# Layer-2 attention: the choice of keys in two DVE steps, the residual added by POOL, the values spread by ACT

## The chip, the cores and the metric

The kernel runs on one core of one Trainium2 chip. The metric is the device time of the whole program, in microseconds (us). The program is a chain of eight layers; the change touches one of them, the attention of layer 2, which takes some 390 us of the span, from about 1682 to about 2070 us.

## The reference, cut to what matters

`x` has 8192 tokens of 128 channels (128 sequences of 64), `ctx` as many. The layer's attention works within one sequence, with 16 heads of 8 channels, and its result is added to `x`:

```python
x = x + _L2_xattn_ref(_layernorm(x, axis=-1), ctx_1024, Wq, Wkv, Wc)

def _L2_xattn_ref(q, kv, Wq, Wkv, Wc):
    qp = einsum('bld,ed->ble', q, Wq)
    idx = argmax(einsum('bld,bmd->blm', qp, kv), axis=-1)   # one context row for each token
    mk, mv = split(einsum('bld,ed->ble', take(kv, idx), Wkv), 2, axis=-1)   # 8 key, 8 value channels
    attn = softmax(einsum('bhld,bmd->bhlm', heads(qp), mk) / sqrt(8))
    return einsum('ble,de->bld', join_heads(einsum('bhlm,bmd->bhld', attn, mv)), Wc)
```

## The kernel before

All of `x` stays in SBUF as 64 tiles of 128 tokens (`k.x`). A tile holds two sequences, four tiles make a group, and there are 16 groups. `phase_l2_attention` gives each engine its own instruction stream, written out by `pipeline` (top of the file): a step n runs, in the order in which the parts are listed, each part on the tile or group n - lag. Nothing reorders a stream: an engine that waits for a semaphore keeps everything listed behind it waiting. Waits go by counters, in tiles.

Parts of every step, for a tile each: PE `score` (L1047, into two PSUM banks), `turn` (transposes the weights, L1056), `project` (L1082) and `weigh` (L1067, L1072); ACT `copy_pT` (L1094) and `exp` (L1088); DVE `centre` (maximum L1100, then subtraction L1103) and `normalise` (reciprocal L1109, product L1112). `score` of a step waits for the subtraction of the step before, because the banks hold one tile's scores.

Parts that run once for a group fall on fixed steps. With n taken modulo 4 they are:

- step 2: DVE `choose`, behind `centre` and `normalise`. It finds each token's chosen key in five stages (maximum L2000, equality L2002, product with a count L2004, minimum L2006, one-hot matrix `hot` L2011) and then signals `hot_ready`. POOL copies the queries (L1881). PE has no group part.
- step 3: PE `turn`, which transposes the normalised input `h` of a later group, and behind it `turn_hot`, which waits for `hot_ready` and transposes `hot` (both L223). ACT copies both results (L1954, L1972). DVE `spread_v` copies the values to their slots (L2025).
- step 0: PE `queries` (L1897) and `values` (L1921). ACT `copy_q` and `norm`, which normalises the next group's input (L1947). DVE `add_x` adds the projected tiles, read from PSUM, to `x` (L1126), then `store_v` (L2017).
- step 1: PE `choose` (L1905, L1909) and `keys` (L1929). DVE `stats_x`, the statistics of the new `x` (L1137, L1142). POOL copies them (L1158). ACT `copy_kvw` (L1966, L1967) and the first half of `spread_k` (L1979); the second half is in step 2.

A new group begins every four steps. Attention proper (`score` to `project`) lags 14 to 17 steps behind the first part of the same group, so that the group parts of later groups run beside the attention of earlier ones. With 64 tiles, `score` runs in the steps 14 to 77, `turn_hot` in the steps 7, 11, ... 67.

Of the kernel before, what the change touches and what calls it, by code (L numbers as in the profile page):

```python
# [14 lines left out]
P = 128  # L15
D = 128
# [25 lines left out]
class Chain:  # L42


    def __init__(self, eng, sem, i=None, per=0):
        self.eng, self.sem, self.i, self.per, self.n = eng, sem, i, per, 0
# [957 lines left out]
class AttentionCore:  # L1004


    def __init__(self, nc, k, ctx, s, name, softmax_scale, bias=None, v_pairs=H // 2):
        def sb(n, shape, dt=F32):
            return ctx.enter_context(nc.sbuf_tensor(f"{name}_{n}", shape, dt))

        self.k, self.s, self.scale, self.bias, self.v_pairs = k, s, softmax_scale, bias, v_pairs
        self.wo = sb("wo", [P, D])
        self.qT = sb("qT", [P, 2, GT])
        self.kbd = sb("kbd", [P, 2, 8, GT])
        self.vbd = sb("vbd", [P, 2, SG, v_pairs, 32])
        self.top = sb("top", [P, H])
        self.prob = sb("prob", [P, 2, H, S])
        self.pT = sb("pT", [P, 2, 8, P])
        self.rec = sb("rec", [P, P])
        self.oT = sb("oT", [P, 2, P])  # L1020
        ps = k.psum
        self.score_banks = (ps[0], ps[1])
        self.scores = k.banks[:, 0:2, :].rearrange("p a (h n) -> p (a h) n", n=S)
        self.pT_banks = (ps[2], ps[3])
        self.oT_psum, self.sum_psum = ps[4][:, 0:P], ps[4][:, P:2 * P]
        self.y_psum = ps[5].rearrange("p (t c) -> p t c", c=D)
# [50 lines left out]
    def project(self, pe, t, r):  # L1077
        s, j = self.s, r % TG
        pe.wait_ge(s.o_ready, t + 1)
        if j == 0:  # L1080
            wait(pe, s.xn_ready, t)
        pe.matmul(self.y_psum[:, j, :], self.oT[:, r % 2], self.wo[:, :], start=True, stop=True).then_inc(s.y_psum, 1)  # L1082

    def exp(self, act, t, r):
# [33 lines left out]
    def add_x(self, dve, t, r):  # L1118
        k, s = self.k, self.s
        if r % TG < TG - 1:  # L1120
            return
        x = k.x[:, bass.ds(t - TG + 1, TG), :]
        dve.wait_ge(s.y_psum, t + 1)
        if self.bias is not None:
            dve.wait_ge(s.biased, t + 1)
        dve.tensor_tensor(x, x, self.y_psum, ALU.add).then_inc(s.xn_ready, TG)  # L1126

    def stats_x(self, dve, t, r):
        k, s = self.k, self.s
# [698 lines left out]
def phase_l2_attention(nc, k):  # L1828
    with ExitStack() as ctx:
        def sb(name, shape, dt=F32):  # L1830
            return ctx.enter_context(nc.sbuf_tensor(f"l2c_{name}", shape, dt))

        s = sems(nc, ctx, "l2a", CORE_SEMS + "var_ready std_ready rstd_ready cleared shift_ready ctx_loaded h_ready hT_psum hT_ready "
                 "q_psum q_copied choice_psum hot_chain hot_ready kvw_ready hotT_psum hotT_ready k_psum v_psum v_copied")
        core = AttentionCore(nc, k, ctx, s, "l2a", float(HD) ** -0.5, v_pairs=2)
        wq = sb("wq", [P, D])
        wkv = sb("wkv", [P, 2 * HD])
        ctxT = sb("ctxT", [P, 2, GT])
# [34 lines left out]
        @block.gpsimd  # L1873
        def _(pool):
            pool.memset(hot[:, :, :].rearrange("p t n -> p (t n)"), 0.0).then_inc(s.cleared, 1)
            core.clear_v(pool, s.cleared)

            def keep_q(at, u):
                pool.wait_ge(s.q_copied, at + TG)
                wait(pool, s.score_psum, at - TG)  # L1880
                pool.tensor_copy(core.qT[:, u, :], q[:, u, :]).then_inc(s.q_ready, TG)  # L1881

            pipeline(pool, k.NT, [(18, lambda t, r: core.copy_mv(pool, t, r)), (10, at_group(keep_q))], unroll=RING, behind=8)

        @block.tensor
        def _(pe):
# [51 lines left out]
        @block.scalar  # L1938
        def _(act):
            finish_stats_act(act, k, s)  # L1940
            act.wait_ge(s.shift_ready, 1)

            def norm(at, u):
                wait(act, s.hT_psum, at)
                settle(act, k)
                for n in range(TG):
                    last = act.activation(h[:, n, :], k.x[:, bass.ds(at + n, 1), :], ACT.Identity, bias=shift[:, bass.ds(at + n, 1)],  # L1947
                                          scale=k.rstd[:, bass.ds(at + n, 1)])
                last.then_inc(s.h_ready, TG)

            def copy_hT(at, u):
                act.wait_ge(s.hT_psum, at + TG)
                wait(act, s.q_psum, at)
                act.copy(hT[:, :], q_bank).then_inc(s.hT_ready, TG)  # L1954

            def copy_q(at, u):
                act.wait_ge(s.q_psum, at + TG)
                wait(act, s.q_ready, at - TG)
                wait(act, s.choice_psum, at - TG)
                act.copy(q[:, u, :], q_bank).then_inc(s.q_copied, TG)  # L1960

            def copy_kvw(at, u):

                act.wait_ge(s.choice_psum, at + TG)
                wait(act, s.k_psum, at)
                act.copy(vw[:, :, :], kvw[:, :, HD:2 * HD])  # L1966
                act.copy(kw[:, :, :, :], kvw[:, :, 0:HD].unsqueeze(2).to_broadcast([P, TG, H, HD])).then_inc(s.kvw_ready, TG)  # L1967

            def copy_hotT(at, u):
                act.wait_ge(s.hotT_psum, at + TG)  # L1970
                wait(act, s.k_psum, at)
                act.copy(hotT[:, :], c_bank).then_inc(s.hotT_ready, TG)  # L1972

            def spread_k(at, u, slots):

                act.wait_ge(s.k_psum, at + TG)
                wait(act, s.score_psum, at - TG)
                for n in slots:
                    last = act.activation(core.kbd[:, u, n, :], q_bank, ACT.Copy, scale=k.headmask8[:, n:n + 1])  # L1979
                return last  # L1980

            pipeline(act, k.NT, [(15, lambda t, r: core.copy_pT(act, t, r)), (14, lambda t, r: core.exp(act, t, r)),
                                 (3, at_group(copy_hT)), (4, at_group(copy_q)), (5, at_group(copy_kvw)), (7, at_group(copy_hotT)),
                                 (9, at_group(lambda at, u: spread_k(at, u, range(0, 4)))),
                                 (10, at_group(lambda at, u: spread_k(at, u, range(4, 8)).then_inc(s.k_ready, TG))),
                                 (0, at_group(norm))], unroll=RING, behind=8)

        @block.vector
        def _(dve):
# [5 lines left out]
            def choose(at, u):  # L1995
                go = lambda ins: ins.then_inc(s.hot_chain, 1)
                wide = lambda ap: ap.unsqueeze(2).to_broadcast([P, TG, S])
                count = k.count128[:, S:P].unsqueeze(1).to_broadcast([P, TG, S])
                dve.wait_ge(s.kvw_ready, at + TG)
                go(dve.tensor_reduce(top[:, :], choice, AX_X, ALU.max))  # L2000
                dve.wait_ge(s.hot_chain, at + 1)
                go(dve.tensor_tensor(marks[:, :, :], choice, wide(top[:, :]), ALU.is_equal))  # L2002
                dve.wait_ge(s.hot_chain, at + 2)
                go(dve.tensor_tensor(marks[:, :, :], marks[:, :, :], count, ALU.mult))  # L2004
                dve.wait_ge(s.hot_chain, at + 3)
                go(dve.tensor_reduce(index[:, :], marks[:, :, :], AX_X, ALU.min))  # L2006
                dve.wait_ge(s.hot_chain, at + 4)
                wait(dve, s.hotT_psum, at)
                for b in range(2):
                    rows = slice(S * b, S * b + S)  # L2010
                    last = dve.tensor_tensor(hot[rows, :, rows], count[rows], wide(index[:, :])[rows], ALU.is_equal)  # L2011
                last.then_inc(s.hot_ready, TG)
# [3 lines left out]
                wait(dve, s.v_ready, at - TG)  # L2016
                dve.tensor_copy(v[:, u].rearrange("p q n -> p (q n)"), c_bank[:, 0:SG * HD]).then_inc(s.v_copied, TG)  # L2017

            def spread_v(at, u):
                dve.wait_ge(s.v_copied, at + TG)  # L2020
                wait(dve, s.o_psum, at - TG)
                for p in range(2):
                    half = slice(64 * p, 64 * p + 64)
                    slots = core.vbd[half, u].rearrange("k q e (f n) -> k q (e f) n", f=2)[:, :, 0:4:3, HD * p:HD * p + HD]
                    last = dve.tensor_copy(slots, v[half, u].unsqueeze(2).to_broadcast([64, SG, 2, HD]))  # L2025
                last.then_inc(s.v_ready, TG)

            pipeline(dve, k.NT, [(14, lambda t, r: core.centre(dve, t, r)), (16, lambda t, r: core.normalise(dve, t, r)),
                                 (17, lambda t, r: core.add_x(dve, t, r)), (6, at_group(choose)), (8, at_group(store_v)),
                                 (18, lambda t, r: core.stats_x(dve, t, r)), (15, at_group(spread_v))],  # L2030
                     unroll=RING, behind=8)


# [1141 lines left out]
```

## Time and profile before

| | us |
|---|---|
| median of 3 runs | 2973.34 (2971.69 to 2976.85) |
| profiled execution | 2975.72 |
| its span, first to last instruction | 2974.2 |
| busy over the span: PE, DVE, ACT, POOL | 2577.0, 2189.5, 1413.7, 440.5 |
| first and last `centre` of layer 2's attention | 1727.0, 2056.4 |

The busy times are sums over eight layers with different limits. The layer of the change has to be read by itself, in order of time.

### The profile page before, as it was taken

The numbers are of one execution on the slowest core, as the hardware profiler recorded it, in microseconds if no ns is written. First come the engines' busy times: TensorE is split into PE (matmuls) and PEld (weight loads), VectorE is DVE, ScalarE is ACT, GpSimd is POOL, SyncE is SP. The second block draws the span as 40 slices with busy tenths as digits, with TensorE's granted clock in tenths as the row PEclk, the third lists the DMA queues.
The fourth block names the chain that finished last, engine by engine and source line by source line (L and its number), as shares of the span: only waits on it lengthen the run. The fifth ranks groups of instructions, "written<-read, shape, count | busy, mean of one in ns | idle before, by whom it ended". The sixth has DMA issues, their size and how long they took to land. (4 is left out here: it accounts for less than half of the span.)

```text
span 2974.2 us, 67297 instructions
## 1 busy us (share of the span) xinstructions
PE 2577.0 (87%) x24798; PEld 1867.2 (63%) x24798; DVE 2189.5 (74%) x5427; ACT 1413.7 (48%) x2523; POOL 440.5 (15%) x542
## 2 busy tenths in 40 slices
PE   5967669995899999999999789896997977999688
PEld 4734346663787887788788456664774744555338
DVE  6889869997577676776776468888881077999774
ACT  3658868885011111111110277774662444777574
POOL 0022210000000000000000000000341163555104
PEclk9988779998899999999999789998998989999799
DMA  3110000001212211211311000000002331000001
GB/s 95 36 65 1 0 20 16 14 14 69 103 58 86 86 58 63 108 57 57 114 57 58 13 16 17 11 8 26 24 30 78 93 89 37 1 0 0 1 0 57
DMA packets 55559, 128.97 MB, mean 43 GB/s; under 512 B 9716, under 2 KB 21460, under 8 KB 54616
## 3 DMA queue, kind: packets, MB, share of 16 engines
q1 hardware_dynamic: 47864, 106.41, 10.4%
q0 software_dynamic: 7520, 20.34, 2.2%
q8 instruction: 97, 1.59, 0.2%
q14 instruction: 78, 0.64, 0.1%
HBM read 109.41 MB, written 17.30 MB: 43 GB/s over the span
## 5 line engine op out<-in xcount | busy, mean ns | idle before, releaser
L1500 PE MATMUL banks<-l1f_feed,l1f_w 128*128 128x512 f32 x512 | 228.5, 597 | 1.4 <-DVE l1f_feed L1769 1.4
L1443 PE MATMUL banks<-l1f_sums,l1f_mixes 128*128 128x256 f32 x768 | 186.6, 379 | 0.0
L1769 DVE TENSOR_TENSOR l1f_feed<-l1f_aoT,l1f_rwb 128x512 f32<-128x512 f32 x256 | 158.8, 682 | 16.2 <-PE banks L1443 10.3
L1500 PEld LDWEIGHTS banks<-l1f_feed,l1f_w 128*128 128x128 f32 x512 | 95.7, 192 | 108.6 <-issue 89.7
L1443 PEld LDWEIGHTS banks<-l1f_sums,l1f_mixes 128*128 128x128 f32 x768 | 145.9, 190 | 19.8
L1443 PE MATMUL banks<-l1f_feed,l1f_mixes 128*128 128x256 f32 x512 | 135.3, 387 | 22.0 <-DVE l1f_feed L1726 22.0
L1735 DVE TENSOR_TENSOR l1f_sums<-l1f_feed 128x512 f32<-128x512 f32 x128 | 88.5, 691 | 87.7 <-PE banks L1443 83.9
L214 POOL COPY x<-xn 128x512 f32 (+1 forms) x16 | 9.8, 610 | 936.4 <-DVE xn L1786 936.4
L1463 PE MATMUL banks<-l1f_w,l1f_feed 128*128 128x128 f32 x1024 | 136.5, 277 | 0.0
L836 POOL TENSOR_TENSOR l3a_kbd<-l_kT,consts 128x1024 f32<-128x1024 f32 x64 | 121.5, 1898 | 64.5 <-PE banks L871 63.8
L1463 PEld LDWEIGHTS banks<-l1f_w,l1f_feed 128*128 128x128 f32 x1024 | 126.0, 194 | 0.0
L1443 PEld LDWEIGHTS banks<-l1f_feed,l1f_mixes 128*128 128x128 f32 x512 | 93.1, 192 | 40.3 <-DVE l1f_feed L1726 26.0
L1602 ACT COPY xb<-banks 128x512 f32<-128x512 f32 x16 | 9.4, 586 | 212.1 <-PE banks L1500 212.1
L1100 DVE TENSOR_REDUCE l2a_top<-banks 128x16 f32<-128x1024 f32 x64 | 78.3, 1223 | 34.4 <-PE banks L1047 33.5
L1720 DVE TENSOR_TENSOR l1f_feed<-l1f_hT,l1f_rwb 128x512 f32<-128x512 f32 x128 | 87.6, 684 | 20.7 <-PE banks L1500 12.6
L1047 PE MATMUL banks<-l2a_kbd,l2a_qT 64*64 64x512 f32 x512 | 71.1, 624 | 35.0 <-DVE l2a_prob L1103 35.0
L1100 DVE TENSOR_REDUCE l1a_top<-banks 128x16 f32<-128x1024 f32 x64 | 77.8, 1216 | 28.9 <-PE banks L1047 28.8
L1158 POOL COPY mean_var<-mvn 128x8 f32 (+1 forms) x32 | 6.1, 191 | 594.1 <-DVE mvn L1142 594.1
L1253 ACT ACTIVATE l1a_kbd<-banks,l1a_bk,consts 128x512 f32<-128x512 f32 x128 | 91.1, 784 | 5.0 <-PE banks L1221 4.9
L2951 DVE TENSOR_TENSOR l2e_y<-banks,l2f_sets 128x512 f32<-128x512 f32 x16 | 11.1, 692 | 110.4 <-PE banks L2918 110.4
L1056 PEld LDWEIGHTS banks<-consts,l2a_prob 128*128 128x128 f32 x512 | 56.0, 143 | 56.4 <-ACT l2a_prob L1088 31.1
L1088 ACT ACTIVATE l2a_prob<-l2a_prob 128x1024 f32<-128x1024 f32 x64 | 68.4, 1069 | 44.9 <-DVE l2a_prob L1103 44.7
(532 smaller groups left out, 7081.0 us busy)
## 6 DMA issues: line engine op xcount, KB each, us to landing
l1f_rwb<-l1f_shares SPq DMA_DIRECT2D x128, 512.0 KB, 6.8
l0a_ctxT<-in_ctxT SPq DMA_DIRECT2D x16, 256.0 KB
l2f_sent<-l0f_zero SPq DMA_DIRECT2D x4, 1024.0 KB, 7.0
l1a_ctxT<-in_ctxT SPq DMA_DIRECT2D x16, 256.0 KB, 2.6
l2c_ctxT<-in_ctxT SPq DMA_DIRECT2D x16, 256.0 KB, 2.6
l2e_rows<-l2f_sent SPq DMA_DIRECT2D x16, 256.0 KB, 2.7
l2f_answers<-l2e_y POOLq DMA_DIRECT2D x16, 256.0 KB, 2.7
l3p_ctxT<-in_ctxT SPq DMA_DIRECT2D x16, 256.0 KB, 2.7
```

The source lines that it names most:

```text
L836: pool.tensor_tensor(kbd[:, par], r.kT[:, bass.ds(P * t, P)].unsqueeze(1).to_broadcast([P, H // 2, P]), k.headmask8.unsqueeze(2).to_broadc ...
L1047: last = pe.matmul(self.score_banks[a][S * b:S * b + S, :], self.qT[rows, u, keys], self.kbd[rows, u, :, keys], start=mask is None, stop=T ...
L1056: last = pe.transpose(self.pT_banks[n // 4][:, P * (n % 4):P * (n % 4) + P], self.prob[:, r % 2, 2 * n:2 * n + 2, :], self.k.ident[:, :])
L1088: act.activation(all_heads, all_heads, ACT.Exp, scale=self.scale).then_inc(s.exp_ready, 1)
L1100: dve.tensor_reduce(self.top[:, :], self.scores, AX_X, ALU.max).then_inc(s.max_ready, 1)
L1253: last = act.activation(core.kbd[:, u, n, :], k_bank, ACT.Identity, bias=bk[:, n:n + 1], scale=k.headmask8[:, n:n + 1])
L1443: return pe.matmul(prods[:, n, :], left, right, start=(p == 0 and first), stop=(p == PAIRS - 1), skip_group_check=True)
L1463: pe.matmul(v_bank[:, D * j:D * j + D], feed[:, at + 1, c:c + P], w[:, 0, e2 if first else e1, :], start=False, stop=(p == PAIRS - 1), ski ...
L1500: pe.matmul(out_bank, w[:, 1, e, :], feed[:, e % NB, :], start=(e == 0), stop=(e == E - 1)).then_inc(s.y_psum, 1)
L1720: dve.tensor_tensor(two(feed[:, at, :]), two(hT[:, m, 0:GT]), halves[:, 0:4:3, :], ALU.mult).then_inc(s.parts_ready, 1)
L1735: dve.tensor_tensor(sums[:, sm, 0:2, :], two(feed[:, at, :]), two(feed[:, at + 1, :])[:, 0:1, :].to_broadcast([P, 2, HT]), ALU.add).then_i ...
L1769: dve.tensor_tensor(feed[:, e % NB, :], aoT[:, m, :], rwb[:, m, e, :], ALU.mult).then_inc(s.ae_ready, 1)
```

## The change

DVE's `choose` keeps its first three stages and stays in step 2. The last two stages (minimum and `hot`, with the signal `hot_ready`) become a new part `place` with lag 7, which is step 3, listed behind `centre` and `normalise`. `spread_v` moves from DVE to ACT, with the same lag (step 3), listed near the end of ACT's step. `add_x` leaves DVE: ACT's new `copy_y` (step 1, first in ACT's list) copies the projected tiles from PSUM to a new SBUF buffer `y_sb`, and POOL's new `add_y_pool` (step 1) adds that to `x`. `project` of a new group waits for `y_copied` in place of `xn_ready`. `stats_x` moves from lag 18 (step 1) to lag 19 (step 2, behind `choose`), and POOL's copy of the statistics from step 1 to step 3.

```diff
 def project(self, pe, t, r):
         if j == 0:
-            wait(pe, s.xn_ready, t)
+            wait(pe, s.y_copied if self.y_sb else s.xn_ready, t)
...
+    def copy_y(self, act, t, r):
+        s = self.s
+        if r % TG == TG - 1:
+            act.wait_ge(s.y_psum, t + 1)
+            wait(act, s.xn_ready, t - TG + 1)
+            act.copy(self.y_sb[0][:, :], self.k.psum[5]).then_inc(s.y_copied, TG)
+
+    def add_y_pool(self, pool, t, r):
+        k, s = self.k, self.s
+        if r % TG == TG - 1:
+            pool.wait_ge(s.y_copied, t + 1)
+            settle(pool, k)
+            x = k.x[:, bass.ds(t - TG + 1, TG), :]
+            pool.tensor_tensor(x, x, self.y_sb[0].rearrange("p (t c) -> p t c", c=D), ALU.add).then_inc(s.xn_ready, TG)
...
-            pipeline(pool, k.NT, [(18, copy_mv), (10, at_group(keep_q))], ...)
+            pipeline(pool, k.NT, [(20, copy_mv), (18, add_y_pool), (10, at_group(keep_q))], ...)
...
-            pipeline(act, k.NT, [(15, copy_pT), (14, exp), ... (0, at_group(norm))], ...)
+            pipeline(act, k.NT, [(18, copy_y), (15, copy_pT), (14, exp), ... (15, at_group(spread_v)), (0, at_group(norm))], ...)
...
 def choose(at, u):
                 go(dve.tensor_tensor(marks[:, :, :], marks[:, :, :], count, ALU.mult))
+
+            def place(at, u):
                 dve.wait_ge(s.hot_chain, at + 3)
                 go(dve.tensor_reduce(index[:, :], marks[:, :, :], AX_X, ALU.min))
                 dve.wait_ge(s.hot_chain, at + 4)
                 wait(dve, s.hotT_psum, at)
                 for b in range(2):
                     last = dve.tensor_tensor(hot[rows, :, rows], count[rows], wide(index[:, :])[rows], ALU.is_equal)
                 last.then_inc(s.hot_ready, TG)
...
             pipeline(dve, k.NT, [(14, centre), (16, normalise),
-                                 (17, add_x), (6, at_group(choose)), (8, at_group(store_v)),
-                                 (18, stats_x), (15, at_group(spread_v))], ...)
+                                 (7, at_group(place)), (6, at_group(choose)), (8, at_group(store_v)),
+                                 (19, stats_x)], ...)
```

## Rows read from the trace of the kernel before

**Rows 1.** Windows: one steady stretch of the stage; busy us and instructions by engine, PEclk, DMA.

```profile
1960.00:1980.00 20.00, 17.87 (x291) 12.51 (x294) 17.66 (x34) 15.30 (x25) 0.80 (x2) 1.00 0.04 13
```

**Rows 2.** Groups by line over the stage: busy us, mean ns | idle before, releaser.

```profile
L1100 DVE TENSOR_REDUCE l2a_top<-banks 128x16 f32<-128x1024 f32 x64 | 78.3, 1223 | 34.4 <-PE banks L1047 33.5
L1047 PE MATMUL banks<-l2a_kbd,l2a_qT 64*64 64x512 f32 x512 | 71.1, 624 | 35.0 <-DVE l2a_prob L1103 35.0
```

**Rows 3.** Timeline, one group from its step 2: start, duration, instruction [idle before].

```profile
1983.66 1.09 PE L1047 MATMUL banks<-l2a_kbd,l2a_qT 64*64 64x512 f32 x8
...
1984.81 1.22 DVE L1100 TENSOR_REDUCE l2a_top<-banks 128x16 f32<-128x1024 f32 x1 [1.17 <-PE banks L1047]
...
1988.40 0.41 DVE L2000 TENSOR_REDUCE l2c_top<-banks 128x4 f32<-128x256 f32 x1
...
1989.77 0.42 DVE L2006 TENSOR_REDUCE l2c_index<-l2c_marks 128x4 f32<-128x256 f32 x1
...
1991.10 1.23 DVE L1100 TENSOR_REDUCE l2a_top<-banks 128x16 f32<-128x1024 f32 x1
...
1991.60 0.60 PE L223 MATMUL banks<-consts,l2c_hot 128*128 128x128 f32 x4
1992.36 1.22 DVE L1103 TENSOR_TENSOR l2a_prob<-banks,l2a_top 128x1024 f32<-128x1024 f32 x1
...
1993.84 1.09 PE L1047 MATMUL banks<-l2a_kbd,l2a_qT 64*64 64x512 f32 x8 [1.64 <-DVE l2a_prob L1103]
...
1999.27 1.09 PE L1047 MATMUL banks<-l2a_kbd,l2a_qT 64*64 64x512 f32 x8
...
2005.31 1.09 PE L1047 MATMUL banks<-l2a_kbd,l2a_qT 64*64 64x512 f32 x8
```

**Rows 4.** Timeline: `stats_x` with DVE work behind it at once, after the last group part.

```profile
2026.18 0.86 DVE L1137 BATCH_NORM_STATS2 bn<-x 128x6 f32<-128x128 f32 x4
...
2027.37 1.19 DVE L1100 TENSOR_REDUCE l2a_top<-banks 128x16 f32<-128x1024 f32 x1
```

**Rows 5.** Timeline: PE waiting for `hot` at the stage's start.

```profile
1697.39 0.85 DVE L2011 TENSOR_TENSOR l2c_hot<-consts,l2c_index 64x256 f32<-64x256 f32 x2
1698.29 0.71 PEld L223 LDWEIGHTS banks<-consts,l2c_hot 128*128 128x128 f32 x4 [2.92 <-DVE l2c_hot L2011]
```

**Rows 6.** Groups by line over the stage: the moved DVE parts, and ACT's smallest and a 128x512 copy.

```profile
L1126 DVE TENSOR_TENSOR x<-x,banks 128x512 f32 x8 | 5.5, 683 | 0.0
L2025 DVE COPY l2a_vbd<-l2c_v 64x128 f32<-64x128 f32 x32 | 6.9, 216 | 0.2
L1966 ACT COPY l2c_vw<-banks 128x32 f32<-128x32 f32 x16 | 3.0, 186 | 30.2 <-PE banks L1929 28.7 <-PE banks L1909 1.5
L1972 ACT COPY l2c_hotT<-banks 128x512 f32<-128x512 f32 x16 | 9.4, 588 | 3.6 <-PE banks L223 3.6
```

**Rows 7.** Groups by line, POOL, whole span: an addition of the same shape in layer 1.

```profile
L1151 POOL TENSOR_TENSOR x<-x,l1a_orow 128x512 f32 x12 | 15.3, 1277 | 2.6 <-issue 1.9
```

**Rows 8.** Timeline, step 1 of one group: `project` on PE, `copy_pT` on ACT.

```profile
1979.57 0.39 PE L1082 MATMUL banks<-l2a_wo,l2a_oT 128*128 128x128 f32 x2
1979.77 1.02 ACT L1094 COPY l2a_pT<-banks 128x1024 f32<-128x1024 f32 x1 [0.55 <-PE banks L1056]
```

**Rows 9.** Windows: PEclk around the stage's last `turn_hot` (columns as in Rows 1).

```profile
2010.00:2015.00 5.00, 3.34 (x66) 2.52 (x62) 4.79 (x9) 3.54 (x6) 0.00 (x0) 1.00 0.01 3
2015.00:2020.00 5.00, 4.50 (x58) 3.46 (x62) 4.20 (x7) 3.20 (x4) 0.00 (x0) 0.69 0.00 0
```

**Rows 10.** Timeline, PE: the stage's first `score`, one `queries`, step 0 after that `turn_hot`.

```profile
1724.97 1.95 PE L1047 MATMUL banks<-l2a_kbd,l2a_qT 64*64 64x512 f32 x8
...
1997.18 1.13 PE L1897 MATMUL banks<-l2c_hT,l2c_wq 128*128 128x512 f32 x2
...
2015.50 1.09 PE L1047 MATMUL banks<-l2a_kbd,l2a_qT 64*64 64x512 f32 x8 [2.06 <-DVE l2a_prob L1103]
...
2021.43 1.09 PE L1047 MATMUL banks<-l2a_kbd,l2a_qT 64*64 64x512 f32 x8
```

More of the change, by code:

```diff
@@ L1004, with __init__ @@
 class AttentionCore:
-    def __init__(self, nc, k, ctx, s, name, softmax_scale, bias=None, v_pairs=H // 2):
+    def __init__(self, nc, k, ctx, s, name, softmax_scale, bias=None, v_pairs=H // 2, pool_adds=False):
         def sb(n, shape, dt=F32):
@@ L1020, in __init__ @@
         self.oT = sb("oT", [P, 2, P])
+        self.y_sb = [sb("y", [P, GT])] if pool_adds else []
         ps = k.psum
@@ L1831, in sb @@
             return ctx.enter_context(nc.sbuf_tensor(f"l2c_{name}", shape, dt))
-        s = sems(nc, ctx, "l2a", CORE_SEMS + "var_ready std_ready rstd_ready cleared shift_ready ctx_loaded h_ready hT_psum hT_ready "
+        s = sems(nc, ctx, "l2a", CORE_SEMS + "y_copied var_ready std_ready rstd_ready cleared shift_ready ctx_loaded h_ready hT_psum hT_ready "
                  "q_psum q_copied choice_psum hot_chain hot_ready kvw_ready hotT_psum hotT_ready k_psum v_psum v_copied")
-        core = AttentionCore(nc, k, ctx, s, "l2a", float(HD) ** -0.5, v_pairs=2)
+        core = AttentionCore(nc, k, ctx, s, "l2a", float(HD) ** -0.5, v_pairs=2, pool_adds=True)
         wq = sb("wq", [P, D])
@@ L1881, in keep_q @@
                 pool.tensor_copy(core.qT[:, u, :], q[:, u, :]).then_inc(s.q_ready, TG)
-            pipeline(pool, k.NT, [(18, lambda t, r: core.copy_mv(pool, t, r)), (10, at_group(keep_q))], unroll=RING, behind=8)
+            pipeline(pool, k.NT, [(20, lambda t, r: core.copy_mv(pool, t, r)), (18, lambda t, r: core.add_y_pool(pool, t, r)), (10, at_group(keep_q))], unroll=RING, behind=8)
         @block.tensor
@@ L1980, in spread_k, with spread_v @@
                 return last
-            pipeline(act, k.NT, [(15, lambda t, r: core.copy_pT(act, t, r)), (14, lambda t, r: core.exp(act, t, r)),
+            def spread_v(at, u):
+                act.wait_ge(s.v_copied, at + TG)
+                wait(act, s.o_psum, at - TG)
+                for p in range(2):
+                    half = slice(64 * p, 64 * p + 64)
+                    slots = core.vbd[half, u].rearrange("k q e (f n) -> k q (e f) n", f=2)[:, :, 0:4:3, HD * p:HD * p + HD]
+                    last = act.copy(slots, v[half, u].unsqueeze(2).to_broadcast([64, SG, 2, HD]))
+                last.then_inc(s.v_ready, TG)
+            pipeline(act, k.NT, [(18, lambda t, r: core.copy_y(act, t, r)), (15, lambda t, r: core.copy_pT(act, t, r)), (14, lambda t, r: core.exp(act, t, r)),
                                  (3, at_group(copy_hT)), (4, at_group(copy_q)), (5, at_group(copy_kvw)), (7, at_group(copy_hotT)),
@@ L1985, in _ @@
                                  (10, at_group(lambda at, u: spread_k(at, u, range(4, 8)).then_inc(s.k_ready, TG))),
-                                 (0, at_group(norm))], unroll=RING, behind=8)
+                                 (15, at_group(spread_v)), (0, at_group(norm))], unroll=RING, behind=8)
         @block.vector
@@ L2004, in choose @@
                 go(dve.tensor_tensor(marks[:, :, :], marks[:, :, :], count, ALU.mult))
+            def place(at, u):
+                go = lambda ins: ins.then_inc(s.hot_chain, 1)
+                wide = lambda ap: ap.unsqueeze(2).to_broadcast([P, TG, S])
+                count = k.count128[:, S:P].unsqueeze(1).to_broadcast([P, TG, S])
                 dve.wait_ge(s.hot_chain, at + 3)
@@ L2017, in store_v @@
                 dve.tensor_copy(v[:, u].rearrange("p q n -> p (q n)"), c_bank[:, 0:SG * HD]).then_inc(s.v_copied, TG)
[L2019 to L2026, printed above, removed]
             pipeline(dve, k.NT, [(14, lambda t, r: core.centre(dve, t, r)), (16, lambda t, r: core.normalise(dve, t, r)),
-                                 (17, lambda t, r: core.add_x(dve, t, r)), (6, at_group(choose)), (8, at_group(store_v)),
-                                 (18, lambda t, r: core.stats_x(dve, t, r)), (15, at_group(spread_v))],
+                                 (7, at_group(place)), (6, at_group(choose)), (8, at_group(store_v)),
+                                 (19, lambda t, r: core.stats_x(dve, t, r))],
                      unroll=RING, behind=8)
```

## The prediction, made before the change was run

> **What bounds the kernel now.** I read the slices by windows first, to see which engine is full in this layer. In a steady stretch of 20 us PE is busy 17.87 us and DVE 17.66 us [rows 1]: neither is clearly the bound, so shares of busy time decide nothing here. The groups by line show that they wait for each other: DVE's maximum lost 34.4 us in the stage, nearly all to `score`, and `score` lost 35.0 us to DVE's subtraction [rows 2]. Which of the two ends last at each step must be read in order of time.
>
> The timeline of one group gives the chain [rows 3]. I count from the `score` of step 2 (1983.66).
> - Step 2: DVE's maximum starts at 1.15, as soon as `score` is through; DVE had been idle 1.17. DVE then works without a break, `choose` from 4.74, until the maximum of step 3 at 7.44.
> - Step 3: the subtraction starts at 8.70 and lasts 1.22; the `score` of step 0 starts 0.26 after it, at 10.18. PE had reached `turn_hot` at 7.94 without waiting, since `hot` was done by then, and sat idle 1.64 before that `score`.
> - Steps 0 and 1: PE sets the time. `score` to `score` takes 5.43 in step 0 and 6.04 in step 1, with no idle time in front of either.
>
> 10.18 + 5.43 + 6.04 = 21.65 us for a group. DVE bounds steps 2 and 3, PE steps 0 and 1. The first 7.4 us are DVE's because `choose` stands in step 2, and PE has 1.64 us to spare in step 3.
>
> **The change part by part.** Durations come from the profiled execution (2975.72 us, 1.5 of it outside the span). It lies 2.4 above the median, so I add differences to the median.
>
> *`choose` cut in two, `stats_x` put behind the first part.* In step 2 the last two stages go, 1991.10 - 1989.77 = 1.33 us, and `stats_x` comes, 1.19 us from its first instruction to the next maximum [rows 3, 4]. Step 2 becomes 0.14 shorter: the maximum of step 3 starts at 7.30. In step 3 `place` may start only behind `centre` and `normalise`, 3.59 us after the maximum (as `choose` does, 1988.40 - 1984.81 [rows 3]): at 10.89. With 1.33 us it ends near 12.2, and `hot_ready` with it. PE gets to `turn_hot` at 7.94 and waits. The hand-over takes 0.05 us (1697.39 + 0.85 to 1698.29 [rows 5]). Behind that wait on PE stands the `score` of step 0, whose own condition, the subtraction, is met at 9.8. The transposes need about 0.5 us before `score` can start (the first pass of 4 covers 0.60 us [rows 3]), so `score` starts at 12.76 where it started at 10.18: 2.58 us later in each group. The next maximum on DVE waits for that `score`.
>
> Nothing in steps 0 and 1 gives it back, for there PE counts, and its work is unchanged. The wait meets a group where `place` falls on a step with `centre` and `normalise`: the steps 19 to 67, 13 groups. 13 x 2.58 = 33.5 us. Step 15 has `centre` but no `normalise` yet, which I put at 1 us; the steps 7 and 11 have neither and cost nothing. From below: if PE's 1.64 us of spare time hid the wait fully, 0. From above: 4.9 (3.59 + 1.33, with nothing absorbed), 64 us. I take 33.5, from the rows of the step itself.
>
> *`add_x` and `spread_v` off DVE.* They free 0.68 and 2 x 0.22 us a group [rows 6]. `add_x` stood in step 0, where DVE next waits for `score`: worth nothing. `spread_v` stood in step 3 behind the subtraction on which `score` depends: worth nothing to PE's chain. `stats_x` leaves step 1, where DVE waited 1.17: nothing either. If the freed 1.13 us all counted, it would be -18 us over 16 groups; that is the other end, and I take 0.
>
> *`copy_y` on ACT.* The new instruction of 128x512 is priced at 0.59 by ACT's copy of that shape [rows 6]. It stands in step 1 before `copy_pT`, in front of which ACT was idle 0.55 [rows 8]: it would end at 1979.22 + 0.59 = 1979.81, and the `project` that now waits for it started at 1979.57. So 0 to 0.3 us a group, 0 to 5 in all. I take 0, because ACT's queue in step 0 starts a little earlier against `score` once DVE waits there. Behind it stand `copy_pT` and `exp`, both with idle time before them.
>
> *`spread_v` on ACT.* Two copies of 64x128; the trace has no such row on ACT, so 0.19 to 0.59 each (128x32 and 128x512 [rows 6]), and I take 0.3. They stand behind `copy_hotT`, which follows the late `turn_hot`, and must end before `weigh` of step 0, over 2 us after its `score`; 0.6 + 0.6 us fit. If not, 0.5 us a group, 8 in all. I take 0.
>
> *`add_y_pool`.* 1.28 us by POOL's addition of the same shape [rows 7]. `stats_x` needs it only at the end of step 2, some 8 us later. POOL's copy of the queries stands behind it and is wanted a group later. The Trainium skill (SBUF — State Buffer, section "SBUF: two separate sides") says that VectorE with two SBUF inputs and GpSimd shut each other out of a shared port pair for a whole instruction. By that rule an addition that met the DVE products of `choose` would hold DVE up to 1.28 us; no run here shows it, since POOL's old parts in this layer are copies. After the last group the longer way counts: 0.59 + 1.28 in place of 0.68, +1 us.
>
> *TensorE's clock.* Before, PE rests 1.64 us at most in the group shown, and the granted clock stayed at 1.00, that is 2.4 GHz [rows 1, 3]. Once it rested 2.06 us, at the last `turn_hot`, and then the mean fell to 0.69, part of the stretch at 1.2 GHz [rows 9, 10]. That step 0 took 5.93 us without `queries`, where a full one less `queries` is 5.43 - 1.13 = 4.30: the fall cost 1.6 us in a stretch bound by PE. In the new order PE rests from 7.94 (0.6 later with the last transposes) to 12.26 in every group, about 4 us. So I expect a fall in each, and all of it counts, since steps 0 and 1 are PE's. Below: 0, if the clock stays. Above: all of step 0 at the ratio 1.95/1.09 of the stage's first `score` [rows 10], 5.43 x 0.79 = 4.3 us. I take 2.0, a little over the one measured fall because the rest is twice as long. 12 groups (the 13th has its fall already) x 2.0 = 24 us; ends 0 and 52. The Trainium skill (TensorE: Matmul & The Clock Gate, section "What's actually happening") says that the throttled state is the default and activity releases it; by that rule the clock falls after each such rest, as forecast.
>
> *Sum:* 33.5 + 24 + 1 (step 15) + 1 (end) = 59.5 us. 2973.3 + 59.5 = **3033 us**, 2.0% slower. A group goes from 21.65 to about 26.2.
>
> **The rivals.**
> - *The wait comes, the clock stays.* 33.5 + 2 = 35.5: **3009 us**. For it: at 1.00 the clock stood rests of 1.64 us. Against: it fell after 2.06.
> - *The clock falls and takes all of step 0 or more.* 33.5 + 2 + 13 x 4.3 = 91: **3065 us**. For it: the stage's first `score` took 1.95 at a time when PE had much to do. Against: after the one fall on record the step two further on is at full speed (`score` 1.09 at 2021.43).
> - *DVE was the bound and is relieved; not slower.* If `place` were done before PE needs it, the 1.13 us a group that leave DVE would become time: 2973 - 18 = **2955 us**. It decides if the part of DVE's step 3 up to `hot_ready` ends before about 9.8 us, when PE could start the next `score`. Against: 7.30 + 3.59 is past that before `place` begins, and DVE is idle in front of the maxima of steps 1 and 2 already. With the same condition and nothing gained, 2973.
> - *POOL and DVE hold each other up.* 16 x 1.28 = 20 on top of the sum: **3053 us**. Against: the addition falls in step 1, while DVE reads PSUM, and the products are in step 2. The page on SBUF named above is where this would come from.
> - *It doesn't do what it says*, in that the addition by POOL comes too late for `stats_x`: 8 us of room against 1.3, so not counted.
>
> **How the numbers follow.** The forecast 0.58, the clock that stays 0.20, the longer fall 0.11, DVE relieved 0.06 (0.04 of it faster, 0.02 no change), POOL against DVE 0.03, and 0.02 for something unseen near the old time. The range goes from 3004, below the case without the fall, to 3058, just short of the longer fall; 0.8 lies in it. Differences under 0.2% (6 us) can't be told from no change here. Faster 0.05, the same 0.03, slower 0.92.
>
> **What would show it.** Right: `turn_hot` waits for DVE's `hot` about 4 us in each group from step 19 on, the idle time in front of `score` in step 0 moves there, DVE's maxima of steps 0, 1 and 2 all wait for `score`; a group lasts 24.2 us plus the clock's share, and PEclk in the stage's windows lies near 0.9. `stats_x` and `add_y_pool` wait for nothing that matters. Wrong: `hot` done when PE arrives, or a group of 21.6 us or less. If PEclk stays at 1.00, the clock term fails and the wait stands alone; if `project` in step 1 waits for `copy_y`, that zero fails.

## The result and the profile after

The changed kernel takes 3037.11 us in the median (4 runs, 3033.49 to 3039.56), the one before 2973.74 (4 runs): 1.0209 times as long, 95% interval 1.0194 to 1.0224. The forecast was 3033, the range 3004 to 3058. The profiled execution took 3033.49 us, its span 3031.8. Line numbers after the change are 1 higher in the attention's parts (`score` L1048, maximum L1101, subtraction L1104), minimum and `hot` are L2036 and L2041, `copy_y` L1134, POOL's addition L1142, `spread_v` L2004.

First, where the time is. From the first maximum of the stage to the last it is 389.12 us (1723.85 to 2112.97), before 329.37 (1727.00 to 2056.37): +59.75; the two profiled executions differ by 57.8. Ahead of the first maximum the layer took 42.0 us in this trace and 44.4 before; it is 41.7 to 42.0 in three of the ten traces (after, e1, v2) and 44.1 to 44.4 in seven; kernels with the moved addition are among both, so this isn't the change. Behind the last maximum it got 1.6 us longer. The last statistics of `x`, before:

```profile
2068.17 0.87 DVE L1137 BATCH_NORM_STATS2 bn<-x 128x6 f32<-128x128 f32 x4 [0.15 <-DVE x L1126]
```

and after:

```profile
2126.41 0.87 DVE L1153 BATCH_NORM_STATS2 bn<-x 128x6 f32<-128x128 f32 x4 [3.11 <-POOL x L1142]
```

They start 11.80 us behind the last maximum before, 13.44 after, where they wait for POOL's addition. The layer as a whole is 59.0 us longer, the other layers together 1.4 shorter. The windows say what kind of loss it is: busy us and (instructions) of PE, PEld, DVE, ACT, POOL, then PEclk, DMA share, GB/s, for 220 us of the stage; before:

```profile
1760.00:1980.00 220.00, 198.53 (x3436) 142.22 (x3438) 194.60 (x356) 165.87 (x257) 7.83 (x20) 1.00 0.04 13
```

and after:

```profile
1760.00:1980.00 220.00, 183.30 (x2848) 127.64 (x2844) 150.18 (x264) 144.92 (x234) 18.03 (x26) 0.89 0.04 11
```

Both PE and DVE are less busy, and PE's clock is down. Each waits for the other more than it did. The waits after, in 1745 to 2090 (us in total, times, longest), name where:

```profile
DVE l2a_top L1101 <- PE banks L1048: 81.2, 40, 3.2
...
PE banks L223 <- DVE l2c_hot L2041: 51.5, 13, 4.6
```

Thirteen waits of 3.96 us in the mean at `turn_hot`, none of which the steady groups of before had. The groups by line over the stage after (busy us, mean ns | idle before, releaser) answer to [rows 2, 6, 7]:

```profile
L1101 DVE TENSOR_REDUCE l2a_top<-banks 128x16 f32<-128x1024 f32 x64 | 77.9, 1218 | 91.1 <-PE banks L1048 91.1
L1048 PE MATMUL banks<-l2a_kbd,l2a_qT 64*64 64x512 f32 x512 | 82.7, 720 | 13.3 <-DVE l2a_prob L1104 13.3
L223 PE MATMUL banks<-consts,l2c_hot 128*128 128x128 f32 x64 | 17.3, 424 | 55.2 <-DVE l2c_hot L2041 55.2
L1142 POOL TENSOR_TENSOR x<-x,l2a_y 128x512 f32 x8 | 10.3, 1284 | 117.7 <-ACT l2a_y L1134 117.7
L2004 ACT COPY l2a_vbd<-l2c_v 64x128 f32<-64x128 f32 x32 | 9.4, 294 | 0.2
```

The maximum's idle time rises from 34.4 to 91.1 us, while its own duration is the same; the idle time in front of `score` falls from 35.0 to 13.3, because that rest now lies in front of `turn_hot` (55.2). A product of `score` has become dearer, 720 ns against 624, with the same work: that is the clock. One group in order of time after, to be laid beside [rows 3]:

```profile
1979.83 1.09 PE L1048 MATMUL banks<-l2a_kbd,l2a_qT 64*64 64x512 f32 x8
1980.99 1.23 DVE L1101 TENSOR_REDUCE l2a_top<-banks 128x16 f32<-128x1024 f32 x1 [2.42 <-PE banks L1048]
...
1985.83 0.86 DVE L1153 BATCH_NORM_STATS2 bn<-x 128x6 f32 x4
...
1987.03 1.19 DVE L1101 TENSOR_REDUCE l2a_top<-banks 128x16 f32<-128x1024 f32 x1
...
1990.59 0.41 DVE L2036 TENSOR_REDUCE l2c_index<-l2c_marks 128x4 f32<-128x256 f32 x1
1991.03 0.85 DVE L2041 TENSOR_TENSOR l2c_hot<-consts,l2c_index 64x256 f32<-64x256 f32 x2
...
1991.94 1.11 PE L223 MATMUL banks<-consts,l2c_hot 128*128 128x128 f32 x4 [4.00 <-DVE l2c_hot L2041]
...
1992.98 1.99 PE L1048 MATMUL banks<-l2a_kbd,l2a_qT 64*64 64x512 f32 x8
1993.62 0.60 ACT L2004 COPY l2a_vbd<-l2c_v 64x128 f32<-64x128 f32 x2
1995.04 1.23 DVE L1101 TENSOR_REDUCE l2a_top<-banks 128x16 f32<-128x1024 f32 x1 [3.15 <-PE banks L1048]
...
2000.14 1.09 PE L1048 MATMUL banks<-l2a_kbd,l2a_qT 64*64 64x512 f32 x8
...
2001.40 0.57 ACT L1134 COPY l2a_y<-banks 128x512 f32<-128x512 f32 x1
2002.11 0.46 PE L1083 MATMUL banks<-l2a_wo,l2a_oT 128*128 128x128 f32 x2
2002.24 1.28 POOL L1142 TENSOR_TENSOR x<-x,l2a_y 128x512 f32 x1 [14.69 <-ACT l2a_y L1134]
...
2006.27 1.09 PE L1048 MATMUL banks<-l2a_kbd,l2a_qT 64*64 64x512 f32 x8
```

Counted from `score` of step 2: maximum of step 3 at 7.20, `hot` done at 12.05, `turn_hot` at 12.11 after a rest of 4.00, `score` of step 0 at 13.15, then 7.16 for step 0 and 6.13 for step 1. A group is 26.44 us here. The reader should see two things at `score` of step 0: it stands behind a wait that is not its own, and it takes 1.99 where the next one takes 1.09; over it (1992.98 to 1994.97) the granted clock is 0.50, that is 1.2 GHz.

### The profile page after: what moved, and what is told of

Its sections match the earlier page's. It is cut to its first block and busy times, and to the rows that moved or that the text cites. A ratio compares the mean times of both kernels' runs of the same rounds, so it can differ in the third digit from the quotient of the medians.

```text
span 3031.8 us, 67318 instructions
## 1 busy us (share of the span) xinstructions
PE 2603.1 (86%) x24798; PEld 1877.6 (62%) x24798; DVE 2173.4 (72%) x5379; ACT 1430.9 (47%) x2571; POOL 460.6 (15%) x558
## 5 line engine op out<-in xcount | busy, mean ns | idle before, releaser
L1101 DVE TENSOR_REDUCE l2a_top<-banks 128x16 f32<-128x1024 f32 x64 | 77.9, 1218 | 91.1 <-PE banks L1048 91.1
L1101 DVE TENSOR_REDUCE l1a_top<-banks 128x16 f32<-128x1024 f32 x64 | 77.8, 1216 | 28.7 <-PE banks L1048 28.7
L1048 PE MATMUL banks<-l2a_kbd,l2a_qT 64*64 64x512 f32 x512 | 82.7, 720 | 13.3 <-DVE l2a_prob L1104 13.3
L1269 ACT ACTIVATE l1a_kbd<-banks,l1a_bk,consts 128x512 f32<-128x512 f32 x128 | 91.1, 784 | 4.9 <-PE banks L1237 4.8
L1095 ACT COPY l2a_pT<-banks 128x1024 f32<-128x1024 f32 x64 | 66.5, 1039 | 48.4 <-PE banks L1057 48.4
L919 ACT ACTIVATE l3a_prob<-l3a_prob 128x1024 f32<-128x1024 f32 x64 | 67.6, 1057 | 45.7 <-DVE l3a_prob L954 45.7
```

The lines of the kernel that those rows point to most:

```text
L919: act.activation(all_heads, all_heads, ACT.Exp, scale=softmax_scale).then_inc(s.exp_ready, 1)
L1048: last = pe.matmul(self.score_banks[a][S * b:S * b + S, :], self.qT[rows, u, keys], self.kbd[rows, u, :, keys], start=mask is None, stop=T ...
L1095: act.copy(self.pT[:, r % 2].rearrange("p a n -> p (a n)"), self.k.banks[:, 2:4, :].rearrange("p a n -> p (a n)"))\
L1101: dve.tensor_reduce(self.top[:, :], self.scores, AX_X, ALU.max).then_inc(s.max_ready, 1)
L1269: last = act.activation(core.kbd[:, u, n, :], k_bank, ACT.Identity, bias=bk[:, n:n + 1], scale=k.headmask8[:, n:n + 1])
```

## The experiments

Three questions. Is the loss the divided choice alone, or do the moved additions and copies have a share? Is it wait and clock, as forecast, or wait alone with something else? And can the division pay if its reader moves along? In the tables, steps run from one DVE maximum to the next, named by the first of the two.

| kernel | median us (runs) | ratio to before, 95% | group | step 2 | step 3 | step 0 | step 1 | PEclk |
|---|---|---|---|---|---|---|---|---|
| before | 2973.74 (4) | | 21.60 | 6.29 | 4.07 | 5.20 | 6.04 | 1.00 |
| after | 3037.11 (4) | 1.0209, 1.0194 to 1.0224 | 26.52 | 6.04 | 8.01 | 6.45 | 6.09 | 0.89 |
| e1, no division | 2980.46 (8) | 1.0025, 1.0015 to 1.0036 | 21.81 | 6.29 | 3.86 | 5.63 | 6.04 | 1.00 |
| e2, division alone | 3020.41 (4) | 1.0157, 1.0141 to 1.0173 | 24.89 | 4.84 | 8.01 | 6.35 | 6.04 | 0.91 |
| e3, PE kept busy | 3019.20 (4) | 1.0146, 1.0130 to 1.0161 | 24.30 | 6.04 | 6.65 | 5.43 | 6.10 | 1.00 |
| e4, `stats_x` in step 1 | 3020.85 (4) | 1.0162, 1.0146 to 1.0177 | 24.95 | 4.84 | 8.03 | 6.25 | 6.04 | 0.92 |
| e5, addition alone | 2979.94 (12) | 1.0021, 1.0011 to 1.0031 | 21.90 | 6.29 | 4.07 | 5.20 | 6.37 | 1.00 |
| v2, later `turn_hot` | 2969.95 (11) | 0.9990, 0.9981 to 0.9999 | 21.25 | 4.84 | 4.91 | 4.75 | 6.84 | 1.00 |
| v3, the same, division alone | 2968.63 (11) | 0.9982, 0.9974 to 0.9991 | 21.07 | 4.84 | 5.40 | 4.78 | 6.04 | 1.00 |
| v4, v3 and `spread_v` on ACT | 2961.57 (6) | 0.9958, 0.9943 to 0.9973 | 20.53 | 4.84 | 4.91 | 4.75 | 6.04 | 1.00 |

The steps are medians over one profiled execution each, the group is the mean of the eleven groups from step 22 on, so the steps need not add up to the group. PEclk is that of 1760 to 1980 us.

### e1: the change without the division

```diff
-   (7, at_group(place)), (6, at_group(choose)), (8, at_group(store_v)), (19, stats_x)
+   (6, at_group(choose)), (6, at_group(place)), (8, at_group(store_v)), (18, stats_x)
```

> The changed kernel with the division of choose taken back: place runs in step 2 right behind choose, stats_x is back in step 1 (lag 18); copy_y, add_y_pool and spread_v on ACT stay as changed. Theory (the late hot_ready holds the score of step 0, the moved parts cost and bring nothing): hot is ready at about 7.4 us after the score of step 2 again, a group lasts 21.4 to 21.7 us, and the time is 2973 plus or minus 5. Rival 1 (the copies on ACT and POOL, or project waiting for y_copied, make the loss): it stays above 3010. Rival 2 (DVE bounds the stage, so the 1.13 us a group that leave DVE are gained): 2955.

The loss of 63 us shrinks to 7. That is outside the 2973 plus or minus 5 that I expected, so the moved additions and copies are not free: together they cost a little, and they gain nothing, though they free DVE of 1.13 us a group. The rival that DVE's work counts one for one falls here, and so does the one that stays above 3010. Between the first maximum and the last it is 3.65 us longer, and the end behind the last maximum 1.3 longer, as in every run with the moved addition; how the rest of the 7 us comes about was not taken apart. A reason for the 3.65 shows in the timeline of a step 0:

```profile
1952.32 1.09 PE L1048 MATMUL banks<-l2a_kbd,l2a_qT 64*64 64x512 f32 x8 [1.54 <-DVE l2a_prob L1104]
1953.64 0.59 ACT L1988 COPY l2c_hotT<-banks 128x512 f32<-128x512 f32 x1
1954.12 0.60 ACT L2004 COPY l2a_vbd<-l2c_v 64x128 f32<-64x128 f32 x2
1954.82 0.67 PE L1068 MATMUL banks<-l2a_pT,consts 128*32 128x128 f32 x16
```

`spread_v` ends at 1954.72, and `weigh` starts 0.1 later, 2.50 after its `score`; where nothing holds it, it starts 2.27 after. So `spread_v` on ACT is late by 0.2 when `score` of step 0 isn't late.

### e2: the division alone, in the kernel before

```diff
-   (17, add_x), (6, at_group(choose)), (8, at_group(store_v)), ...
+   (17, add_x), (7, at_group(place)), (6, at_group(choose)), (8, at_group(store_v)), ...
```

> The kernel before with the division of choose alone: place in step 3 behind centre and normalise; add_x, stats_x and spread_v stay on DVE where they were. Theory: the maximum of step 3 comes 1.33 us earlier (6.1 after the score of step 2), place ends 4.9 us after it at 11.0, so the score of step 0 starts near 11.6 instead of 10.2: 13 x 1.4 = 18 us for the wait. PE rests about 3 us, the clock falls in each group, 12 x 2 = 24 us more: 3015. If the clock stays at this shorter rest: 2992. Rival (the division is harmless, the moved additions and copies make the loss): 2980 or less.

The division by itself costs 47 us, though no work is added; the rival of 2980 or less falls. I had expected 3015, 18 of it for the wait and 24 for the clock; which of the two is larger than that was not measured here. PE in one group (`turn_hot`, and `score` of step 0 behind it):

```profile
1808.07 0.99 PE L223 MATMUL banks<-consts,l2c_hot 128*128 128x128 f32 x4 [2.89 <-DVE l2c_hot L2016]
1808.99 1.99 PE L1047 MATMUL banks<-l2a_kbd,l2a_qT 64*64 64x512 f32 x8
1815.66 1.09 PE L1047 MATMUL banks<-l2a_kbd,l2a_qT 64*64 64x512 f32 x8
```

The rest is 2.89 us instead of 4.00, and the clock still falls: `score` 1.99, PEclk 0.91 in the stage.

### e4: the change with `stats_x` back in step 1

```diff
-   (19, lambda t, r: core.stats_x(dve, t, r))
+   (18, lambda t, r: core.stats_x(dve, t, r))
```

> The changed kernel with stats_x put back into step 1 (lag 18); the division and all else stay. Theory (DVE's work between the score of step 2 and hot_ready counts one for one): 1.19 us less in that chain, hot_ready at 10.9 instead of 12.1, 13 x 1.19 = 15 us gained; PE still rests near 3 us and the clock still falls: 3020. If the clock does not fall at this rest: 2996. Rival (DVE's load as such counts, wherever it stands): no difference, 3037.

The time falls by 16.3 us to that of e2, as expected (3020). The wait at `turn_hot` shrinks from 51.5 us in 13 times to 37.4:

```profile
PE banks L223 <- DVE l2c_hot L2041: 37.4, 13, 3.5
```

Step 2 loses 1.20, one for one: DVE's chain from the maximum of step 2 to `hot` is what PE waits for, and `stats_x` (1.20 us, 1985.83 to 1987.03 in the group above) stood in it for nothing. So going from before over e2 and e4 to the change, the division takes 46.8, the moved addition and `spread_v` 0.4, which is within the spread of four runs each, and `stats_x` 16.3. These are differences in a row, so their sum has to come out and proves nothing. Nor do the parts have fixed prices: the moved ones cost 7 us in e1, where nothing else makes PE wait longer, and nothing that can be seen once the division does.

### e3: the wait without the rest

```diff
 def turn_hot(at, u):
+    # groups whose attention runs: six products into an idle bank, nobody reads them
+    pe.wait_ge(s.pT_ready, at - 7)
+    for _ in range(6):
+        pe.matmul(k.psum[2][:, 0:2 * P], k.ident, k.consts[:, 0:2 * P], start=True, stop=True)
     ...  # wait for hot_ready, transposes
```

> The changed kernel with work added: in front of the wait of turn_hot PE computes 6 matrix products of 128x256 for nothing (about 3.2 us, into a PSUM bank that is free then), from step 15 on, so that it rests under 1 us while it waits for hot. Theory (the wait and the clock are two terms): the granted clock stays at 1.00 through the stage, hot_ready is as late as before, and of the loss only the wait is left: 3008 to 3014. Rival (the fall of the clock costs nothing, the wait and other parts make the whole loss): 3037, or more where the products run over the wait.

PE works where it rested, and `hot` comes as late as in the kernel after. One step 3 and step 0:

```profile
1850.36 1.19 DVE L1101 TENSOR_REDUCE l2a_top<-banks 128x16 f32<-128x1024 f32 x1
...
1851.39 2.86 PE L1932 MATMUL banks<-consts 128*128 128x256 f32 x12 [0.18 <-ACT l2a_pT L1095]
1853.91 0.41 DVE L2040 TENSOR_REDUCE l2c_index<-l2c_marks 128x4 f32<-128x256 f32 x1
1854.36 0.85 DVE L2045 TENSOR_TENSOR l2c_hot<-consts,l2c_index 64x256 f32<-64x256 f32 x2
1855.27 0.66 PE L223 MATMUL banks<-consts,l2c_hot 128*128 128x128 f32 x4 [1.01 <-DVE l2c_hot L2045]
1855.85 1.09 PE L1048 MATMUL banks<-l2a_kbd,l2a_qT 64*64 64x512 f32 x8
```

From the maximum of step 3 to the end of `hot` it is 4.85 us, as in the kernel after (1987.03 to 1991.88). But the transposes are through in 0.58 (1855.27 to 1855.85; after: 1.04) and `score` takes 1.09. The window of the stage is back at full clock:

```profile
1760.00:1980.00 220.00, 203.97 (x3160) 146.49 (x3160) 163.38 (x289) 156.03 (x254) 18.27 (x27) 1.00 0.04 12
```

So the two costs come apart. From first to last maximum e3 takes 363.66 us, 34.3 more than before, and the kernel after 25.5 more than e3. Of e3's 34.3, 2.6 fall in the first four steps, where the kernel after has 0.9: there the added products themselves cost 1.7. Without these, the wait is 32.6 us and the clock 27.2. Step by step against before, e3 gives +2.6 to 2.8 in step 3 in each of the 13 groups from step 18 on, the kernel after +3.93 to 3.96. The 1.36 on top is the transposes and `score` at the lower level (1.2 instead of 2.4 GHz; 0.46 and 0.90), and 0 to 1.5 more come in step 0.

The whole program gained less than that, 17.9 us instead of 25.5, so the median of 3019 missed the expected 3008 to 3014; the rival of 3037 falls all the same. The excess lies outside the stage, in layers that the edit does not touch: the last layer took 80.7 us in the profiled execution instead of 73.8, the layer-2 feed-forward 452.4 instead of 449.0. In the last layer of e3 one DVE product shows it:

```profile
2960.62 1.23 DVE L2554 TENSOR_SCALAR l3d_f<-l3d_f 128x2048 f32<-128x2048 f32 x1 [0.44 <-ACT l3d_f L2541]
...
2965.83 2.55 DVE L2554 TENSOR_SCALAR l3d_f<-l3d_f 128x2048 f32<-128x2048 f32 x1 [1.45 <-ACT l3d_f L2541]
2966.00 1.28 POOL L206 TENSOR_TENSOR xb<-x,l3f_b_out 128x512 f32<-128x512 f32 x1
```

1.23 us alone; 2.55 with an addition of POOL of 1.28 us beside it. In this layer of e3 such an addition runs beside 7 of the 16 products, and these seven take 2.44 to 2.55; it runs beside one of the 16 before and one after (2.45 and 2.44), and all others take 1.23. Six more of 1.3 are 7.8 us, about the 6.9 by which the layer is longer. The 3.4 of the feed-forward were not traced. Three of the four runs of e3 lie near 3019, one at 3012.07, so how these meet may differ between executions; only one was profiled.

### e5: the addition by ACT and POOL alone

```diff
+   ACT:  (18, copy_y), ...
+   POOL: (20, copy_mv), (18, add_y_pool), ...
-   DVE:  (17, add_x), ...
```

`choose`, `spread_v` and `stats_x` as before.

> The kernel before with the addition alone moved (copy_y on ACT, add_y_pool on POOL, POOL's copy of the statistics in step 3); choose is whole in step 2, stats_x in step 1, spread_v on DVE. Without the division the moved parts still lost 0.25%. Theory (spread_v on ACT ends after the point where weigh of step 0 wants it, 0.2 us in each of 13 groups, and the rest is the longer end, 0.59 + 1.28 for 0.68): about half of the 7 us comes back, 2976, the group 21.6 as before. Rival (copy_y holds project in step 1): no gain, 2980.

My 2976 missed, the rival was right. Step 1 of a group:

```profile
1936.66 1.09 PE L1048 MATMUL banks<-l2a_kbd,l2a_qT 64*64 64x512 f32 x8
1938.16 0.56 ACT L1134 COPY l2a_y<-banks 128x512 f32<-128x512 f32 x1
1938.87 0.46 PE L1083 MATMUL banks<-l2a_wo,l2a_oT 128*128 128x128 f32 x2
```

`project` follows the end of `copy_y` by 0.15 and its `score` by 2.21; where nothing holds it, it follows `score` by 1.95. Step 1 grows by 0.33. DVE's 0.68 bought nothing that shows, and the copy that replaces it stands before `project` on PE's own step.

### v2, v3, v4: the reader of `hot` moved behind as well

v2 edits the kernel after, v3 the kernel before with e2's division:

```diff
 PE:
-   (3, at_group(turn)), (4, at_group(queries)), (5, at_group(choose)), (7, at_group(turn_hot)), ...
+   (3, at_group(turn)), (8, at_group(turn_hot)), (4, at_group(queries)), (5, at_group(choose)), ...
 ACT:
-   (15, copy_pT), (14, exp), ..., (7, at_group(copy_hotT)), ...
+   (15, copy_pT), (8, at_group(copy_hotT)), (14, exp), ...
 v2 also, DVE:
-   (19, stats_x)
+   (18, stats_x)
```

`turn_hot` now stands in step 0, behind that step's `score` instead of in front of it.

> The changed kernel with stats_x in step 1 and the waiting part moved too: PE's turn_hot goes from step 3 to step 0 (lag 8), behind weigh and before queries, and ACT's copy of it to step 0 between copy_pT and exp. Theory (the division was right for DVE, and it lost only because turn_hot stood in front of the score of step 0): hot is ready 4.9 us after the maximum of step 3, turn_hot comes up 6.1 after it and waits for nothing; from maximum to maximum 4.84 in step 2, 6.04 in step 1, steps 3 and 0 together 9.8; a group 20.7 instead of 21.6, 13.5 x 0.9 = 12 us gained on the kernel before, 3 lost at the end: 2964. Rival (PE bounds steps 0 and 1, half a microsecond more there is paid in full and nothing comes back): 2980.

> The kernel before with choose divided (place in step 3) and turn_hot with its copy in step 0, as in the run beside it; add_x, stats_x and spread_v stay on DVE where they were. Theory: the same chain, 20.7 us a group, since the parts left on DVE stand where it waits for PE, and the end is not longer: 2961. Rival (DVE needs to be relieved for the division to pay): it stays at 2974 or falls behind the run beside it by 5 or more.

Both are faster than before, v2 only just (its interval ends at 0.9999), both by less than expected, and for different reasons. Their rivals (2980 for v2, no gain for v3) fall. In v2 `project` waits for `copy_y` (6.84 in step 1, e5's loss in a larger size):

```profile
1912.57 0.46 PE L1083 MATMUL banks<-l2a_wo,l2a_oT 128*128 128x128 f32 x2 [0.59 <-ACT l2a_y L1134]
```

In v3 `spread_v` stands on DVE behind `place`, and `weigh` of step 0 waits for it:

```profile
1924.25 0.85 DVE L2016 TENSOR_TENSOR l2c_hot<-consts,l2c_index 64x256 f32<-64x256 f32 x2
1925.13 0.46 DVE L2030 COPY l2a_vbd<-l2c_v 64x128 f32<-64x128 f32 x2
1925.69 0.67 PE L1067 MATMUL banks<-l2a_pT,consts 128*32 128x128 f32 x16 [0.51 <-issue]
```

The profile puts those 0.51 down to issue; `spread_v` ends at 1925.59, 0.1 before `weigh` starts, and v4 tests it, v3 with `spread_v` on ACT as in the change:

```diff
+   ACT: ..., (15, at_group(spread_v)), (0, at_group(norm))
-   DVE: ..., (18, stats_x), (15, at_group(spread_v))
+   DVE: ..., (18, stats_x)
```

> The kernel before with three edits: choose divided (place in step 3), turn_hot with its copy in step 0, and spread_v on ACT; add_x and stats_x stay on DVE in steps 0 and 1, no copy_y. In the two runs with turn_hot in step 0, one group took 21.07 us because spread_v on DVE came behind place and held weigh of step 0 about 0.5 us, the other 21.25 because project in step 1 waited 0.6 to 0.8 us for copy_y. Theory: with neither of these a group takes 9.66 (steps 3 and 0) + 6.04 + 4.84 = 20.55 us, 13.5 x 1.05 = 14 us under the kernel before: 2960. Rival (add_x and store_v on DVE in step 0 then bound it): 2968, as the better of the two.

2961.57 us (expected 2960), 0.42% faster than before and 2.5% faster than the change. The group of v4:

```profile
1906.00 1.09 PE L1047 MATMUL banks<-l2a_kbd,l2a_qT 64*64 64x512 f32 x8
...
1912.00 1.22 DVE L1100 TENSOR_REDUCE l2a_top<-banks 128x16 f32<-128x1024 f32 x1
...
1914.62 1.09 PE L1047 MATMUL banks<-l2a_kbd,l2a_qT 64*64 64x512 f32 x8 [0.51 <-DVE l2a_prob L1103]
1915.58 0.41 DVE L2020 TENSOR_REDUCE l2c_index<-l2c_marks 128x4 f32<-128x256 f32 x1
...
1916.02 0.85 DVE L2025 TENSOR_TENSOR l2c_hot<-consts,l2c_index 64x256 f32<-64x256 f32 x2
...
1917.96 0.66 PE L223 MATMUL banks<-consts,l2c_hot 128*128 128x128 f32 x4
...
1920.44 1.09 PE L1047 MATMUL banks<-l2a_kbd,l2a_qT 64*64 64x512 f32 x8
...
1926.48 1.09 PE L1047 MATMUL banks<-l2a_kbd,l2a_qT 64*64 64x512 f32 x8
```

`hot` is done at 1916.87, 1.1 before PE reaches `turn_hot`: no wait. The maximum of step 3 comes 6.00 after `score` of step 2 instead of 7.44, since `place` is off DVE's step 2; `score` of step 0 at 8.62 instead of 10.18, and PE's rest there is 0.51 instead of 1.64. PE's clock stays at 1.00. The division was not wrong; the place of its reader was. What `turn_hot` in step 0 brings without the division, with `choose` whole in step 2, was not run.

## Why the prediction was right, point by point

- **The wait.** Forecast 2.58 a group and 33.5 in all. e3 has the wait without the fall of the clock. There `score` of step 0 comes 12.75 us after that of step 2, in the mean from step 22 on; forecast 12.76. From maximum to maximum it is 31.7 over the 13 groups, and 33.1 without step 68, where e3 is 1.4 shorter because the one fall of before [rows 9] is gone there. The two terms that make it, step 2 shorter by 0.14 and `hot` near 12.2, were 0.24 shorter (7.20 instead of 7.44) and 12.05. Right. The same step had a price inside it that I netted away: `stats_x`, put where `place` had been, takes back 1.20 of the 1.33 that left. e4 shows that it alone cost 16 us, because DVE's step 2 is on the path: without it PE rests some 2.9 us instead of 4.0, as in e2.
- **The clock.** Forecast 2.0 a group, 24 us, from the one fall of before [rows 9, 10]. Measured 27.2 for 13 falls, by e3; the last stands for the one of before, which leaves about 25.8 against the 24. So a fall costs 2.1 in the mean, a little over the 1.6 of before. The clock falls in each group, PEclk is 0.89 (forecast near 0.9), the rest 4.00 (about 4). Shown by e3, where `hot` comes as late and the clock stays. That the size fits is partly luck: single falls cost 1.4 to 2.8, and the 2.0 came from a single one after a shorter rest; that a rest twice as long costs a little more was assumed, and no run tests it by itself. `score` of step 0 stands at 13.15 where I put 12.76, because the transposes ahead of it run at the lower level too (1.04 against my 0.5); the sum has no term of its own for this. The Trainium skill (TensorE: Matmul & The Clock Gate, section "What's actually happening") says that the throttled state is the default and activity releases it; the trace agrees in every group.
- **Step 15 and the end.** Forecast 1 and 1. The first four steps give +0.9. The end is 1.6 longer, 13.44 for 11.80 from the last maximum to the last statistics: 1.3 by the longer way over ACT and POOL, as in e1, e4 and e5 (13.1), and 0.3 because the last `project` takes 0.80 instead of 0.49, at the lower clock. Right, a little too small.
- **`add_x` and `spread_v` off DVE, worth 0.** Right that nothing is gained: e1, without the division, is slower than before, not faster; the other end, -18, is ruled out. The rival of 2955 falls.
- **`copy_y`, 0 taken, 0.3 the upper bound.** Right for this kernel: step 1 grew by 0.05 (6.09 for 6.04), because `score` of step 0 is late and ACT is ahead. In other orders it is wrong: 0.33 in e5, about the upper bound, and 0.8 in v2. Its cover was the loss itself.
- **`spread_v` on ACT.** Forecast 0.3 each, measured 0.294; not late in the kernel after, late by 0.2 in e1.
- **`add_y_pool`.** Forecast 1.28, measured 1.284. The rival that POOL and DVE hold each other up falls for this layer: DVE's subtraction that starts beside the addition of 2002.24 takes 1.23, as elsewhere, and e4 and e2 differ by 0.4 us.
- **The sum.** 3033 forecast, 3037.11 measured; a group 26.2 forecast, 26.52 measured. The two profiled executions differ by 57.8 against my 59.5, and the median of the kernel after lies 3.6 above its own profiled execution: most of the 4 us left is the spread of the runs. Term by term the wait is 0.4 under its forecast, the clock 1.8 over and the end 0.6 over; in the profiled execution the shorter start of the layer (2.4) and the other layers (1.4) hide that.

## What to carry to other kernels

Cutting a part in two to relieve an engine moves the wait of whoever reads its result. Look at what is queued behind that reader on its in-order engine: here `score` stood behind transposes that it did not need. With the transposes behind it, and `spread_v` on ACT, the same division gains 0.4% where it cost 1.6%. When the waiting engine is TensorE, price the rest twice: for its length (here 32.6 us), and for the lower clock at which the work behind it runs if the clock falls (here 27.2).

## What the runs showed of the hardware

- TensorE's clock fell from 2.4 to 1.2 GHz in each group after rests of 2.8 to 2.9 us (e2, PEclk 0.91; `score` behind them 1.74 to 1.99 instead of 1.09) as it did after 4.0 (0.89), and in none of the 13 where PE rested 0.7 to 1.0 us behind work of 2.86 (e3, 1.00). The part of the cost in step 3 is the same in nearly every group (1.36 us), that in step 0 is not: in the kernel after step 0 is longer than before by 0.2, 1.0, 1.4 and 1.7 us in four groups running (steps 20 to 32) and by 0.3, 1.1, 1.5 and 1.7 in the next four; e3 has 0.2 to 0.3 there throughout. What sets this wasn't tried.
- A DVE product of 128x2048 in SBUF doubles from 1.23 to 2.55 us when an addition of POOL of 1.28 us starts beside it, in e3's last layer: seven times there, and never without one. The Trainium skill (SBUF — State Buffer, section "SBUF: two separate sides") says that VectorE in a 2-port mode and GpSimd lock a shared port pair for a whole instruction; the 1.32 us added here are about the POOL instruction's length, so the trace agrees in size. By that section of the Trainium skill the first to start keeps the pair; in the trace DVE starts 0.06 to 0.17 ahead and is the one that is lengthened, so who took it first is not seen. In the layer of the change, with the addition beside a DVE subtraction that reads PSUM, the subtraction's mean stays at 1224 ns.
